# Switch layer routed in groups of 9, 9, 13 and 5 tiles, with the end of the kernel written out and the dense steps regrouped

## The reference, cut to what matters

```python
def _L1_ffn_ref(x, switch_w, switch_b, expert_w, expert_b):
    CAPACITY_FACTOR = 1.2
    B, S, D = x.shape                    # 8, 576, 128
    E = switch_w.shape[0]                # 16
    N = B * S
    xf = x.reshape(N, D)
    logits = xf @ switch_w.T + switch_b
    probs = jax.nn.softmax(logits, axis=-1)
    route_probs = jnp.max(probs, axis=-1)
    routes = jnp.argmax(probs, axis=-1)
    oh = jax.nn.one_hot(routes, E, dtype=jnp.int32)
    pos = jnp.take_along_axis(jnp.cumsum(oh, axis=0), routes[:, None], axis=1)[:, 0] - 1
    capacity = int(CAPACITY_FACTOR * N / E)
    keep = pos < capacity
    buf = jnp.zeros((E, capacity, D), dtype=xf.dtype).at[routes, pos].set(xf)
    y = jnp.einsum('ecd,efd->ecf', buf, expert_w) + expert_b[:, None, :]
    gathered = y[routes, jnp.minimum(pos, capacity - 1)]
    out = jnp.where(keep[:, None], gathered, xf) * route_probs[:, None]
    return out.reshape(B, S, D)
...
x = x + _L0_conv_ref(_ln_c(x), ...)      # then a mixture of experts, both before the stages spoken of here
x = x + _L1_conv_ref(_ln_c(x), ...)      # softmax attention over the 576 tokens of each of 8 images
t = _to_tokens(x)
t = t + _L1_ffn_ref(_ln_t(t), ...)       # the Switch layer: one of 16 experts for each token
```

## Time and profile before

| what | us |
|---|---|
| median of the runs (lowest to highest of 3) | 453.77 (451.72 to 454.06) |
| span of the profiled execution | 475.2 |
| DVE busy in the span | 307.1 |
| PE busy in the span | 378.1 |
| last result added by the experts' DVE work (L1376) | 413.91 |
| first gather issued by POOL (L1117) | 416.77 |
| last add to `R` begins its group of nine (L1357) | 470.27 |

### The profile page before, as it was taken

One profiled execution on the slowest core, in us unless ns is written; L12 is line 12 of the kernel. 1 busy time (PEld: TensorE's weight loads), 2 busy tenths in 40 slices (PEclk: granted clock), 3 DMA queues, 4 the chain that ended last, 5 costly groups with the idle time before them and its releaser, 6 DMA issues.

```text
span 475.2 us, 6675 instructions
## 1 busy us (share of the span) xinstructions
PE 378.1 (80%) x2125; PEld 318.0 (67%) x2125; DVE 307.1 (65%) x952; ACT 153.9 (32%) x324; POOL 126.6 (27%) x141
## 2 busy tenths in 40 slices
PE   6954949869999999987479999988965947987071
PEld 5954939748878888874369999978865616842030
DVE  5747857775655565695665868657639376476287
ACT  2221344452333323322144555746353202310000
POOL 4830360028000000030005621010445730077700
PEclk9997555569999999998557999999987589998676
DMA  9921500009000000000210011110000145622213
GB/s 180 278 86 21 184 0 1 1 33 415 18 0 1 0 0 0 0 0 2 51 25 9 24 33 33 31 33 2 24 28 23 50 141 178 241 62 73 60 55 99
DMA packets 22906, 29.66 MB, mean 62 GB/s; under 512 B 4120, under 2 KB 18265, under 8 KB 22622
## 3 DMA queue, kind: packets, MB, share of 16 engines
q1 hardware_dynamic: 18366, 22.47, 16.2%
q0 software_dynamic: 1728, 3.54, 2.5%
q10 hardware_dynamic: 2784, 3.29, 2.0%
HBM read 13.48 MB, written 12.78 MB: 55 GB/s over the span
## 4 chain that ended last, share of the span: by engine, by line
PE 24%; DVE 18%; another core or an unknown queue 4%; issue 3%; ACT 3%; DMA 1%; POOL 0%; SPq 0%; DVEq 0%; ACTq 0%
DVE R L1368 9%; PE ps L1585 6%; PE ps L1553 3%; PE ps L1679 2%; PE ps L1565 2%; PE ps L1607 2%; PE ps L1633 1%; DVE R L1357 1%; PE ps L1572 1%; DVE mx L1177 1%; PE ps L1599 1%; DVE K L1192 1%; ACT sH L1434 1%; PE ps L1698 1%
## 5 line engine op out<-in xcount | busy, mean ns | idle before, releaser
L155 POOL TENSOR_TENSOR rstd<-sm,neg_half 128x9 f32<-128x9 f32 x12 | 21.7, 1810 | 204.8 <-DVE sm L149 204.6
L804 PE MATMUL ps<-wide,gu_w 128*128 (+1 forms) x108 | 52.2, 483 | 2.4 <-PEq L701 2.4
L1585 PE MATMUL ps<-V,wide 128*128 128x129 f32 x400 | 52.7, 280 | 0.0
L876 ACT ACTIVATE s<-ps 128x384 f32<-128x384 f32 (+1 forms) x60 | 29.5, 492 | 68.2 <-PE ps L808 67.9
L835 PE MATMUL ps<-h,wd 128*128 128x384 f32 x120 | 50.2, 500 | 1.6 <-DVE h L920 1.2
L1368 DVE SCALAR_TENSOR_TENSOR R<-ps,dense_w,R 128x128 f32<-128x128 f32 x144 | 39.3, 343 | 18.7 <-remote 5.7
L1585 PEld LDWEIGHTS ps<-V,wide 128*128 128x128 f32 x400 | 49.6, 196 | 0.0
L915 DVE TENSOR_TENSOR t<-ps,s 128x384 f32<-128x384 f32 x48 | 26.7, 557 | 30.8 <-ACT s L876 30.6
L1177 DVE TENSOR_REDUCE mx<-ps 128x1 f32<-128x576 f32 (+1 forms) x40 | 29.9, 751 | 12.0 <-PE ps L1553 11.8
L808 PE MATMUL ps<-wide,gu_w 128*128 (+1 forms) x108 | 37.2, 345 | 0.3 <-DVE t L915 0.3
L805 PE MATMUL ps<-wide,gu_w 128*128 (+1 forms) x108 | 37.2, 345 | 0.0
(11 more groups left out here) (206 smaller groups left out, 831.2 us busy)
## 6 DMA issues: line engine op xcount, KB each, us to landing
slots<-zrow SPq DMA_DIRECT2D x7, 768.0 KB, 7.7
xe<-slots SPq DMA_DIRECT2D x16, 192.0 KB, 3.9
slots<-wide ACTq DMA_DIRECT2D x16, 192.0 KB, 2.6
xall<-in_x SPq DMA_DIRECT2D x8, 288.0 KB, 6.7
out<-R SPq DMA_DIRECT2D x12, 192.0 KB
Q<-sQK SPq DMA_DIRECT2D x8, 144.0 KB, 2.4
K<-sQK SPq DMA_DIRECT2D x8, 144.0 KB, 2.5
ew<-in_ew SPq DMA_DIRECT2D x1, 1024.0 KB, 5.4
```

The lines of the kernel that those rows point to most:

```text
L804: nc.tensor.matmul(o, gu_w[0][:, w], xTH[:, at], start=True, stop=False)
L876: nc.scalar.activation(s4[q][:r], bank[q][:r, :CH], ACT.Silu).then_inc(s_ok[q], 1)
L1585: last = nc.tensor.matmul(bank[6 + k // 3][:, k % 3 * (C + 1):(k % 3 + 1) * (C + 1)], PT[n % 2][:, jk, i0:i0 + P], V[n % 2][:, jk, :], sta ...
```

## The change

The routing groups become tiles 0 to 8, 9 to 17, 18 to 30 and 31 to 35. The third holds nine sent tiles and four dense ones, all of whose attention is complete one image before the end; the fourth holds the last five dense tiles. All loops end with the last image, and what followed is written out by hand. The statistics of group 2 no longer wait for a free buffer, since the last two groups have buffers of their own. The last router chunk of group 1 goes into another bank, and is transposed before the projection of the last image. Group 0 is counted two blocks earlier in its image.

The dense tiles are regrouped in four sets of 2, 2, 2 and 3 tiles, so 16 steps in place of 12. Four steps stand ahead of the experts and 12 behind them. The expert stage has two banks for transposes and two for products in place of four and four. The biases of the dense tiles are added in two pieces (four and five tiles), and the `combine` of a part stands behind step 10 and each of steps 11 to 14, and four behind the end.

```diff
-        SPLIT = 3
-        LAST = B + 5
+        SPLIT = 5
...
-        BEHIND = 5
-        DENSE_AT, WT_AT = ((1, 2, 3), (5, 6, 7)), (0, 4, 1)
-        TR_AT, YE_AT = (0, 4, 1, 2), (3, 5, 6, 7)
+        TR_AT, YE_AT = (2, 3), (4, 5)
...
+        GROUP = ((0, 9), (9, 18), (18, 31), (31, 36))
+        TAIL = ((18, 21), (21, 24), (24, 27), (27, 31), (31, 34), (34, 36))
+        TAIL_AT = (2, 3, 2, 3, 2, 3)
+        SETS = ((27, 28), (29, 30), (31, 32), (33, 34, 35))
+        STEPS = [(k, q) for k in range(len(SETS)) for q in range(4)]
+        def step_banks(j):
+            k = STEPS[j][0]
+            if len(SETS[k]) == 2:
+                return ((0, 1), (6, 7))[j % 2]
+            return ((0, 1, 2), (6, 7, 3))[j % 2]
...
         def l_bank(g, c):
-            return bank[0] if c == 2 and 2 * g + 5 > B else bank[4 + c % 2]
+            return bank[2] if (g, c) == (1, 2) else bank[4 + c % 2]
...
                 rstd6(0)
                 rstd6(1)
                 scatter(0, range(GT))
-                rstd6(2)
+                rstd_tail(2)
                 scatter(1, range(0, SPLIT))
-                rstd6(3)
+                rstd_tail(3)
                 scatter(1, range(SPLIT, GT))
                 scatter(2, range(GT))
...
+                dve.wait_ge(o_ok, NB_SS * (B - 1))
+                moments_tail(2, stats_tail(DENSE0, GROUP[2][1]))
+                route_max(1)
+                route_first(1)
+                route_slot(1)
+                place_counts(1, bank[5])
+                place_sums(1)
+                place_index(1)
+                attended(B - 1, (0, 1, 2))
+                attended(B - 1, (3, 4))
+                dve.wait_ge(o_ok, NB_SS * B)
+                moments_tail(3, stats_tail(*GROUP[3]))
+                add_bias_tail(2)
+                route_max(2)
+                route_first(2)
+                route_slot(2)
+                place_counts(2, bank[5])
+                place_sums(2)
+                place_index(2)
+                weigh_dense(2)
...
+                add_step(0)
+                add_step(1)
+                add_bias_tail(3)
+                route_max(3)
+                route_first(3)
+                add_step(2)
+                place_counts(3, bank[5])
+                place_sums(3)
+                weigh_dense(3)
+                add_step(3)
+                experts7(0, E1)
...
+                add_step(10)
+                combine(0)
+                add_expert_bias(DENSE0, 31, 5, 1)
+                add_step(11)
+                combine(1)
...
+                add_step(15)
+                add_expert_bias(31, 35, 4, 2, last=False)
+                add_expert_bias(35, NT, 5, 2)
+                for part in range(5, ROUTED * 3):
+                    combine(part)
```

More of the change, by code:

```diff
@@ L1401, in _, with add_expert_bias @@
-                for part in range(12 - BEHIND, ROUTED * 3):
+                def add_expert_bias(first, end, b, done, last=True):
+                    dve.wait_ge(b9, done)
+                    dve.wait_ge(s9, count)
+                    ins = nc.vector.tensor_tensor(R[:, first:end, :], R[:, first:end, :],
+                                                  bank[b][:, :(end - first) * C].rearrange("p (t c) -> p t c", c=C), ALU.add)
+                    if last:
+                        ins.then_inc(d8o, 1)
@@ L1634, in dense, with transposes_tail @@
                                                 ew[:, 4 * quad:4 * quad + 4, :].rearrange("c e f -> c (e f)"),
                                                 start=True, stop=True)
-                    if tiles3[-1] == 2:
-                        last.then_inc(q9, 1)
+                    last.then_inc(q9, 1)
+                def transposes_tail(c):
+                    pe.wait_ge(xnT, c + 1)
+                    if c >= 2:
+                        pe.wait_ge(cpT, c - 1)
+                    first, end = TAIL[c]
+                    for t in range(first, end):
+                        last = nc.tensor.transpose(bank[TAIL_AT[c]][:, (t - first) * P:(t - first + 1) * P], tail_xn(t), ident)
+                    last.then_inc(trT, 1)
@@ new lines, in logits_tail @@
+                def logits_tail(c):
+                    pe.wait_ge(cpT, c + 1)
+                    first, end = TAIL[c]
+                    base = GROUP[2 if c < 4 else 3][0]
+                    for t in range(first, end):
+                        last = nc.tensor.matmul(bank[4][:, (t - base) * E1:(t - base + 1) * E1],
+                                                tail_xT(c)[:, (t - first) * P:(t - first + 1) * P], rt1[:],
+                                                start=True, stop=True)
+                    last.then_inc(lcT, 1)
@@ L1669, in _ @@
                         maxima_row(n + 1)
-                    if g is not None:
-                        logits(g, 2)
+                    if g == 0:
+                        logits(0, 2)
                     transposes(n)
+                for k in range(3):
+                    attend(B - 1, k)
+                counts(1, bank[5])
+                for k in range(3, NB_SS):
+                    attend(B - 1, k)
+                pe.wait_ge(lg_ok, 6)
+                transposes_tail(0)
+                transposes_tail(1)
@@ new lines, in _ @@
+                logits_tail(0)
+                transposes_tail(2)
+                logits_tail(1)
+                transposes_tail(3)
+                logits_tail(2)
+                logits_tail(3)
+                pe.wait_ge(pt_ok, NB_SS * B)
+                dense(0)
+                pe.wait_ge(cr6, 2)
+                counts(2, bank[5])
+                pe.wait_ge(o_ok, NB_SS * B)
+                dense(1)
+                transposes_tail(4)
+                transposes_tail(5)
+                pe.wait_ge(bsT, 1)
@@ new lines, in expert_bias @@
+                def expert_bias(first, end, b, done=True):
+                    for t in range(first, end):
+                        last = nc.tensor.matmul(bank[b][:, (t - first) * P:(t - first + 1) * P],
+                                                wT[:, (t - DENSE0) * P:(t - DENSE0 + 1) * P], ebr[:], start=True, stop=True)
+                    if done:
+                        last.then_inc(b9, 1)
+                for j in range(4, 9):
+                    dense(j)
+                pe.wait_ge(ye7, E1)
@@ L1726, in metaformer_kernel @@
+                for j in range(13, 16):
+                    dense(j)
         local.close()
```

473 lines of the change are left out of this document (281 added, 192 removed).

## The result

The changed kernel takes 451.77 us (median) against 453.76, a ratio of 0.9946 with a 95% interval of 0.9922 to 0.997. The ratio is worked out from all runs of both kernels but the few in a slower state. That is 0.5% faster, some 2.4 us by the ratio and 2.0 by the medians; the forecast was 447.4, 6.4 us. The profiled execution of after took 448.98 us with a span of 446.8.

The account below looks back on a forecast made before the run. The end was taken as three stages: POOL's scatters, the expert loads and experts, then DVE's adds. 2.5 us won up to the last expert add and 3.9 behind it made 6.4: 453.8 to 447.4, range 443.5 to 455.

Parts of the forecast that it names:

- The expert stage: 16 experts' transposes and products on PE: 16.9 us from the first load's landing plus 1.4, done at 402.5 against 405.0.
- The cleaning of the trace: Idle gaps of 23.6 us taken out of before's 475.2 us span, leaving 451.6; gains then put under the median of 453.8.
- the four gaps: Idle times in before's end, taken to belong to the profiled execution alone: 2.87, 3.50, 2.52 and 14.72 us.
- The check against the median: The span less the gaps, 451.6 us, compared with the runs' median of 453.8: 2.2 us under it.
- The scatter stage: POOL's 18 scatters and power, 24.96 us: start at 354.3 against a cleaned 356.95, last scatter ending at 379.2 to 379.9.
- the scatter comes no sooner: Rival: the 13-tile chain is 2 to 3 us late, experts start as before, 450 to 451.5 us; chance 0.14.
- Dense steps ahead: Four dense steps before the experts end at 381 to 383, hidden by the scatter with 1 to 3 us to spare.
- ring of two: Two banks must not slow the experts, margin 0.3 us; as a rival, 5.6 us lost, 453.0, chance 0.11.
- the cold start: Start of the experts on PE: 1.4 us added since PE will have idled.
- Behind the experts: DVE's adds, combines and waits from the last expert add to the end: 42.7 us against 46.6, 3.9 won.
- The floor set by the gathers: Behind the experts: gathers land at 38.4 us, DVE wants the last at about 39.4; 41.7 is the least possible.
- the rival with the slow clock: PE works the 12 dense steps behind the experts at 1.2 GHz: 458.5 to 463.3 us; chance 0.08.

Follow-up runs that it names:

- 2nd trace: The kernel before, unchanged, profiled a second time: 450.23 us, span 448.3, without the four gaps.
- the kernel with the gap put in: The kernel before with 10 extra ACT copies of 128 columns ahead of the last V copy (2.69 us): 458.42 us, ratio 1.0103.
- the first trace of before: The kernel before, unchanged, the profiled execution the prediction was made from: span 475.2 us, 151.61 from the common attend products to the end.
- six ahead: The kernel after with 6 of the 16 dense steps ahead of the experts in place of 4, and 10 behind: 448.55 us, ratio 0.9893.
- third trace: The kernel before, unchanged, profiled a third time: 459.63 us, 131.44 from the common attend products to the end.
- the two traces of after: The kernel after, unchanged, profiled twice: 448.98 us, then 448.46 us.

## Why the prediction was wrong

Its terms against the traces, in us from the common products (323.60 taken off the forecast's times):

| | before: forecast | before: 2nd trace | after: forecast | after: traces | won: forecast | won: traces |
|---|---|---|---|---|---|---|
| group 1's first scatter | 33.35 | 31.88 | 30.7 | 31.29 | 2.65 | 0.6 |
| last scatter ends | 58.3 | 56.80 | 55.6 to 56.3 | 56.83 | 2.0 to 2.7 | 0 |
| last expert add ends | 81.4 | 80.10 | 78.9 | 80.36, 80.00 | 2.5 | -0.3 to 0.1 |
| from there to the end | 46.6 | 45.52 | 42.7 | 43.98, 43.91 | 3.9 | 1.5 to 1.6 |
| all | 128.0 | 125.62 | 121.6 | 124.34, 123.91 | 6.4 | 1.3 to 1.7 |

Before was 2.4 us quicker than it was taken to be, and after is 2.3 to 2.7 slower than the sum: 1.3 to 1.4 of that in the expert stage and 1.2 to 1.3 behind it.

**The cleaning of the trace** is the step that failed first: 2.4 us of the 4.7 to 5.1 that are missing. That the four gaps belong to that one execution was right; the second trace has none. But they were taken out by the length of their idle time, 23.6 us, and together they cost 26.0: 4.34 for the 2.87 of the first, 5.8 for the 6.02 of the second and third, 15.8 for the 14.72 of the fourth. For the first, the kernel with the gap put in shows the rest: PE's clock falls by the end of its wait, and the transposes, attend products and router products behind it run at the low level. The row for it stood in the first trace of before, an attend block of 2.36 us where others take 1.28:

```profile
349.06 2.36 PE L1585 MATMUL ps<-V,wide 128*128 128x129 f32 x10
```

Why the fourth cost 1.1 more was not tried; a dense step behind it takes 5.18 us, 2.84 in the second trace. The Trainium skill ("TensorE: Matmul & The Clock Gate", section "HAM oscillation — how this bites in real kernels") tells of waits for data that let the clock drop and of products that then pay for it; the stretch at 0.57 behind the first gap agrees, and the prediction had used that page for the end only, not for the gaps.

**The check against the median** was the second failure of the same step. That 451.6 came out 2.2 under the median was taken to go with a clean trace (a run's time lies some 2 us over its span: 450.23 and 448.3). The median holds what the runs lose themselves: the common products start up to 4.3 us later in some traces than in others. An undisturbed execution of before takes 450.2, so the agreement was chance.

**The scatter stage.** POOL back to back was right for before (24.96 and 24.92 us). For after the start was 0.6 too early, and the wait for the 13-tile list, at most 0.7 by the forecast, was 1.86. This is the rival "the scatter comes no sooner", which had 0.14 and named ACT's turns of copies and normalising: with these taken apart the wait went. This cost PE nothing against the forecast: its first transposes stand 3.8 and 3.6 us behind the last scatter, where the sum had 4.6, so they begin at 60.67 and 60.39, and 60.6 was put. Dense step 0 ahead of the counts, its other reason, costs some 0.2: the counts start at 364.34, and the one-hot was there at about 364.15.

**Dense steps ahead.** That they are hidden was right: DVE ends them 2.1 us ahead of PE's first transposes (381.1 and 383.18), within the 1 to 3 of the forecast, and 6.3 us ahead of its own first expert add, so two more fit. That they were on the path before was wrong: PE took the third expert late because the second and third gap had held DVE up. Undisturbed, the 16 expert adds take 15.5 to 15.8 us in both kernels, and there was nothing to win.

**The expert stage** is a term that was too small, by 1.3 to 1.4 us. From PE's first transposes to the last expert add it takes 19.7 and 19.6 us, and the sum had 18.3. 1.0 us each and a ring of two that doesn't slow it were right: 0.44 idle ahead of each add. The start was wrong: the sum let the first product follow one expert's transposes and a copy, 0.9 us, but PE takes the transposes of three experts first and waits for the third load, so the first product comes 2.69 us behind the first transposes (2.27 in the second trace). With six ahead, where the clock is at 1.00, it still comes 2.50 behind them, and the stage takes 18.5; so the cold start is worth 1.1 to 1.2, for which 1.4 was put.

**Behind the experts.** The adds of DVE were priced well: 1.65 us of waits are left, and 0.64 at the start where 0.75 was put. The floor set by the gathers was not: 41.7 by the forecast, 43.9 in the trace. They take 35.4 us for 34 (a gather of 2.35 among those of 0.95), and the last lands 2.4 us after its issue ends, not 1.5. So the chain that was "covered, but only just" ends last. In before the stage took 45.5 and not 46.6: of the 3.1 us of waits between later steps only 1.4 are there (the 1.36 above), so less could be won.

**The clock behind the experts** stayed at 1.00 in the steps of two tiles, from 402 to 434 in after; the rival with the slow clock didn't come. In before it does fall there in some executions: the 47.26 of its third trace, and the same 47.26 in the kernel with the gap. Against these after wins 3.3 us in this stage, against the undisturbed one 1.5. How often each comes in runs without a trace, and so what part of the 2.0 to 2.4 us it makes up, stays open.

## What to carry to other kernels

A gap that one execution alone shows can cost more than its idle time, as the first did here, when TensorE runs slowly behind it, or no more, as the second and third: look at the products behind it too, against the same products elsewhere in the trace, or better, run the kernel again and compare stage by stage from a common instruction. A median that agrees with a cleaned trace proves nothing while runs differ among themselves by more than the effect. Where two chains of nearly one length end together, shorten both: here, by the medians, 18 gathers fewer gave 1.2 us, two steps moved gave 3.2, and both gave 7.1 (by the traces 0 to 0.4, 1.0 to 1.5, and 5.3 to 5.7).

## What was unexpected of the hardware

A wait of 3.99 us on PE, where it was 1.45 before, brought the granted clock from 1.00 to 0.57 in the next stretch, and 2.69 us of ACT's work became 4.12 us of delay.

The record of the clock and the time don't always go together. From 60 to 75 us the two traces of after show 0.50 and 1.00, with the same busy time of PE, and the common products start at 322.51 in both:

```profile
60.00:75.00 15.00, 8.28 (x40) 7.61 (x39) 8.66 (x40) 6.43 (x16) 7.73 (x4) 0.50 0.00 1
```

```profile
60.00:75.00 15.00, 8.29 (x39) 7.63 (x39) 8.66 (x40) 6.63 (x17) 7.73 (x4) 1.00 0.00 1
```

So a mean clock of 0.865 and one of 0.934 stand beside 448.98 and 448.46 us. It is the products' own durations that tell whether a stretch was slow; behind the gap they do (2.36 us for 1.28).
